# Gated attention stage: where a pair's projections and maxima stand among its sixteen units

## The reference

```
ss = sigmoid(x @ Ws).reshape(b, t, H, E); sd = sigmoid(x @ Wd).reshape(b, t, H, E)   # H = 8, E = 5
ss_g = ss * top3_mask(ss); sd_g = sd * top3_mask(sd)
q = sum over experts of (x @ Wq)[.., H, E, 64] * sd_g;  k, v likewise from Wkv with ss_g
attn = softmax(q k^T / 8);  out = attn v                       # per block b of 4 and head h of 8
y = sum over experts of (out @ Wo)[.., E, 128] * mask(sd)
```

## Time and profile before

| | |
|---|---|
| median of 3 runs | 4347.36 us |
| profiled execution | 4350.9 us, span 4349.2 us, mean granted clock 0.955 |
| PE busy | 3864.7 us (89%) |
| DVE busy | 3243.0 us (75%) |
| ACT busy | 1925.3 us (44%) |
| POOL busy | 2938.9 us (68%) |
| gated stage, units of pairs 0 to 15 | from 1282.3 to 2516 us of the span |

### The profile page before, as it was taken

One profiled execution on the slowest core, in us unless ns is written; L12 is line 12 of the kernel. 1 busy time (PEld: TensorE's weight loads), 2 busy tenths in 40 slices (PEclk: granted clock), 3 DMA queues, 4 the chain that ended last, 5 costly groups with the idle time before them and its releaser, 6 DMA issues. The chain is left out here.

```text
span 4349.2 us, 63343 instructions
## 1 busy us (share of the span) xinstructions
PE 3864.7 (89%) x22554; PEld 2205.7 (51%) x22554; DVE 3243.0 (75%) x5670; ACT 1925.3 (44%) x3478; POOL 2938.9 (68%) x2166
## 2 busy tenths in 40 slices
PE   7999999999788889899899848999999999999964
PEld 4555555555455555555555424555455444545533
DVE  6876878868487777877876648887888788878826
ACT  3443444434355455455455313444444444434423
POOL 3776767667536777877787835777677677767740
PEclk8999999999889999999999968999999999999987
DMA  3000100000010000100100021221222121212121
GB/s 55 21 22 1 38 14 25 10 6 1 27 59 20 28 19 28 38 19 28 33 28 10 6 59 30 41 34 30 39 32 43 30 40 30 43 22 44 19 59 30
DMA packets 98073, 125.90 MB, mean 29 GB/s; under 512 B 28928, under 2 KB 76480, under 8 KB 97760
## 3 DMA queue, kind: packets, MB, share of 16 engines
q1 hardware_dynamic: 97760, 121.86, 13.2%
HBM read 103.69 MB, written 18.12 MB: 28 GB/s over the span
## 5 line engine op out<-in xcount | busy, mean ns | idle before, releaser
L845 POOL TENSOR_TENSOR s_psum_p<-s_psum_p,s_prob 128x1024 f32<-128x1024 f32 (+3 forms) x640 | 1336.9, 2089 | 387.0 <-ACT s_prob L550 336.7
L550 ACT ACTIVATE s_prob<-s_sT 128x1024 f32<-128x1024 f32 (+2 forms) x896 | 792.0, 931 | 842.9 <-DVE s_sT L701 474.1
L449 PE MATMUL s_pv<-s_prob,s_vp 128*64 128x512 f32 (+3 forms) x3584 | 798.9, 567 | 3.9 <-POOL s_prob L830 3.9
L657 DVE CUSTOM_DVE_ANT_0 s_mx<-s_mx,s_strip 128x512 f32<-128x512 f32 x628 | 422.0, 714 | 161.8 <-PE s_mx L406 159.1
L1734 POOL TENSOR_TENSOR s_psum_p<-s_psum_p,s_prob 128x1024 f32<-128x1024 f32 x192 | 462.1, 2407 | 108.0 <-ACT s_prob L1457 106.2
L1457 ACT ACTIVATE s_prob<-s_sT 128x1024 f32<-128x1024 f32 x256 | 262.7, 1026 | 581.5 <-PE s_sT L1321 581.4
L706 DVE RECIPROCAL s_recip<-s_recip 128x128 f32<-128x128 f32 x512 | 452.7, 922 | 34.8 <-ACT s_recip L497 34.8
L406 PE MATMUL s_mx<-s_bh,s_ah 64*128 64x512 f32 (+2 forms) x1756 | 396.7, 447 | 87.2 <-DVE s_bm L647 39.0
L845 POOL TENSOR_TENSOR s_psum_p<-s_prob 128x1024 f32<-128x1024 f32 (+1 forms) x128 | 288.1, 2251 | 204.7 <-ACT s_prob L550 202.0
L449 PEld LDWEIGHTS s_pv<-s_prob,s_vp 128*64 128x64 f32 x3584 | 219.3, 137 | 369.0 <-issue 289.2
L647 DVE TENSOR_REDUCE s_bm<-s_mx 128x6 f32<-128x768 f32 (+2 forms) x376 | 360.0, 957 | 53.3 <-PE s_mx L406 44.6
(11 more groups left out here) (291 smaller groups left out, 7418.7 us busy)
## 6 DMA issues: line engine op xcount, KB each, us to landing
s_strip<-bias_rows SPq DMA_DIRECT2D x256, 144.0 KB, 5.8
s_wr<-gated_weights SPq DMA_DIRECT2D x32, 960.0 KB, 4.9
s_near<-bias_rows SPq DMA_DIRECT2D x256, 48.0 KB, 2.0
x<-s_x SPq DMA_DIRECT2D x10, 512.0 KB, 3.2
s_x<-x SPq DMA_DIRECT2D x8, 512.0 KB, 4.7
gated_weights<-s_side_hi SPq DMA_DIRECT2D x8, 480.0 KB, 2.6
gated_weights<-s_side_lo SPq DMA_DIRECT2D x8, 480.0 KB, 2.9
s_x<-in_L_attn_x_dram SPq DMA_DIRECT2D x4, 512.0 KB, 5.4
```

Of the source, the lines that this page charges most:

```text
L449: last = mm(pv[heads(hd), lo:CH], vp[:, g % 2, j, heads(hd)], prob[:, k % PR, hd, lo:CH], start=j == 0, stop=end)
L550: nc.scalar.activation(prob[:, k % PR, :, lo:CH], sT[:, k % 2, :, lo:CH], ACT.Exp, scale=st.scale).then_inc(exp_done, 1)
L657: last = nc.vector.tensor_tensor_reduce(out=mx[:, hd, :], in0=mx[:, hd, :], in1=strip[:, g % 2, hd, first:first + CH], scale=1.0, scalar=N ...
L845: nc.gpsimd.tensor_tensor(out[:, :, lo:CH], src, p[:, :, lo:CH], ALU.add)\
```

## The change

Both counts are rewritten: two projection steps in each of units 0 to 7, and maxima steps one each in units 4 and 5 and two each in units 8 to 14. The transposition of the maxima goes from unit 14 to unit 15 and stands right behind the scores there. In a unit, the projections now come ahead of the first maxima step, on TensorE and on VectorE, and no maxima step borrows a score buffer any more. The masked products of the first half (zp 0 to 3) go from units 12 to 15 to units 13, 14, 15 and 15. The gating of the next block (gx, gl) goes from units 6 to 9 to units 12 to 15; the ranking, which was in six groups of three or more operations spread over two pairs, is cut into 16 steps of one operation, all in the ranked pair from unit 5 on. The layer norm's steps move by one to three units.

```
--- before.py
+++ after.py
@@ -52,7 +52,7 @@
 ROWS = 16
 NROW = P // ROWS
 RINGP = 5
-TOPS, TOPC = E0 + 1, 8 + 3 * (E0 - 1)
+TOPS, TOPC = 4 + 3 * (E0 - 1), 8 + 3 * (E0 - 1)
 
 
 class Pairs:
@@ -939,8 +939,9 @@
 
     def __init__(self, name, scale):
         super().__init__(name, False, False, scale)
-        self.mx_steps = [0] * 4 + [1] * 6 + [2, 2, 3, 3, 0, 0]
-        self.pj_steps = [2] * 4 + [1] * 8 + [0] * 4
+        self.mt_unit = 15
+        self.mx_steps = [0] * 4 + [1, 1, 0, 0] + [2] * 7 + [0]
+        self.pj_steps = [2] * 8 + [0] * 8
         self.NP = HF // 2
         self.GP = B * self.NP
 
@@ -969,17 +970,16 @@
                 out[3 + i].append(("zp", g - 1, i))
         out[10].append(("rs", 2 * g))
         out[11].append(("zt", g, 0))
-        for i in range(4):
-            out[12 + i].append(("zp", g, i))
+        for i, u in enumerate((13, 14, 15, 15)):
+            out[u].append(("zp", g, i))
         gated, ranked = {0: 1, 3: 2, 7: 3}.get(g), {1: 1, 4: 2, 8: 3}.get(g)
         if gated is not None:
-            for u, job in ((6, ("gx", gated, 0)), (7, ("gx", gated, 1)), (8, ("gl", gated, 0)),
-                           (9, ("gl", gated, 1)), (10, ("top", gated, 0)), (11, ("top", gated, 1)),
-                           (14, ("top", gated, 2))):
+            for u, job in ((12, ("gx", gated, 0)), (13, ("gx", gated, 1)), (14, ("gl", gated, 0)),
+                           (15, ("gl", gated, 1))):
                 out[u].append(job)
         if ranked is not None:
-            for k, u in enumerate((8, 9, 11)):
-                out[u].append(("top", ranked, 3 + k))
+            for n, u in enumerate((5, 5, 6, 7, 8, 8, 9, 9, 10, 11, 11, 12, 12, 13, 14, 15)):
+                out[u].append(("top", ranked, n))
         if p == 0 and b > 0:
             for u, job in ((6, ("gt", b - 1, 0)), (7, ("gt", b - 1, 1)), (8, ("gt", b - 1, 2)),
                            (9, ("gt", b - 1, 3)), (12, ("y", b - 1, 0)), (13, ("gt", b - 1, 4)),
@@ -992,7 +992,7 @@
         if p == 1 and b + 1 < B:
             for k in range(2):
                 out[12 + k].append(("xs", b + 1, k))
-        for n, (of, u) in enumerate(((1, 13), (1, 14), (1, 15), (2, 2), (2, 3), (2, 6), (2, 7))):
+        for n, (of, u) in enumerate(((1, 15), (1, 15), (2, 4), (2, 5), (2, 6), (2, 6), (2, 9))):
             if p == of and b > 0:
                 out[u].append(("ln", b - 1, n))
         return out
@@ -1351,11 +1351,13 @@
                 scores(g, u, k, c, j)
                 steps = [t for t in todo if t[0] == "pj"]
                 chunks = [t for t in todo if t[0] == "mx"]
-                early = 1 if steps else 2
-                for t in chunks[:early]:
-                    maxima(t[1], t[2], second(todo, t, k))
+                early = 1
+                if ("mt", g + 1) in todo:
+                    m_transpose(g + 1)
                 for n, t in enumerate(steps):
                     project(t[1], t[2], k if n == 0 else None)
+                for t in chunks[:early]:
+                    maxima(t[1], t[2])
                 for t in todo:
                     if t[0] in GMISC:
                         misc_job(t)
@@ -1363,8 +1365,6 @@
                     values(k - 2)
                 for t in chunks[early:]:
                     maxima(t[1], t[2])
-                if ("mt", g + 1) in todo:
-                    m_transpose(g + 1)
             for k in range(GP * U - 2, GP * U):
                 values(k)
             for t in ending:
@@ -1575,34 +1575,36 @@
                 dve.wait_ge(xh_done, 2 * b + c + 1)
                 tt(xl[:, half(c)], xT[:, half(c)], f32(xh[:, half(c)]), ALU.subtract).then_inc(xl_done, 1)
 
-            def top_experts(b, k):
+            def top_experts(b, n):
 
                 gates, kept = gate[:, b % 2, :, :], keep[:, :, :]
-                at = TOPC * b + E0 + 3 * (k - 1)
-                if k == 0:
+                k, part = divmod(n + 2, 3)
+                if n == 0:
                     dve.wait_ge(sig_done, 2 * b + 2)
                     for e in range(E0):
                         nc.vector.memset(kept[:, e, :], float(E0 - 1 - e)).then_inc(top_step, 1)
-                elif k < E0:
+                    return
+                dve.wait_ge(top_step, TOPC * b + E0 + n - 1)
+                if k < E0:
                     later, earlier, won = slice(k, E0), slice(0, E0 - k), beats[:, 0:E0 - k, :]
-                    dve.wait_ge(top_step, at)
-                    tt(won, gates[:, earlier, :], gates[:, later, :], ALU.is_ge).then_inc(top_step, 1)
-                    dve.wait_ge(top_step, at + 1)
-                    tt(kept[:, later, :], kept[:, later, :], won, ALU.add).then_inc(top_step, 1)
-                    dve.wait_ge(top_step, at + 2)
-                    tt(kept[:, earlier, :], kept[:, earlier, :], won, ALU.subtract).then_inc(top_step, 1)
+                    if part == 0:
+                        ins = tt(won, gates[:, earlier, :], gates[:, later, :], ALU.is_ge)
+                    elif part == 1:
+                        ins = tt(kept[:, later, :], kept[:, later, :], won, ALU.add)
+                    else:
+                        ins = tt(kept[:, earlier, :], kept[:, earlier, :], won, ALU.subtract)
+                elif part == 0:
+                    ins = nc.vector.tensor_scalar(kept, kept, float(TOP) - 0.5, None, ALU.is_lt)
+                elif part == 1:
+                    ins = tt(gates, gates, kept, ALU.mult)
                 else:
-                    dve.wait_ge(top_step, at)
-                    nc.vector.tensor_scalar(kept, kept, float(TOP) - 0.5, None, ALU.is_lt)\
-                        .then_inc(top_step, 1)
-                    dve.wait_ge(top_step, at + 1)
-                    tt(gates, gates, kept, ALU.mult).then_inc(top_step, 1)
                     if b >= 2:
                         dve.wait_ge(share_done, 2 * NP * (b - 1))
-                    nc.vector.tensor_copy(
+                    ins = nc.vector.tensor_copy(
                         keep_d[:, b % 2, :, :, :],
-                        kept.rearrange("p e (i s h) -> p e i s h", i=NB, s=2)[:, :, :, 1, :])\
-                        .then_inc(top_step, 1)
+                        kept.rearrange("p e (i s h) -> p e i s h", i=NB, s=2)[:, :, :, 1, :])
+                ins.then_inc(top_step, 1)
+                if n == TOPS - 1:
                     dve.wait_ge(top_step, TOPC * (b + 1))
                     dve.sem_inc(top_done, 1)
 
@@ -1683,19 +1685,19 @@
                     misc_job(t)
                 steps = [t for t in todo if t[0] == "pj"]
                 chunks = [t for t in todo if t[0] == "mx"]
-                early = chunks[:1] if steps else chunks[:2]
-                for t in early:
-                    maxima(t[1], t[2], second(todo, t, k))
+                early = chunks[:1]
+                if ("mt", g + 1) in todo:
+                    max_rows(g + 1)
                 for n, t in enumerate(steps):
                     project(t[1], t[2], k if n == 0 else None)
+                for t in early:
+                    maxima(t[1], t[2])
                 for t in todo:
                     if t[0] == "mx":
                         if t not in early:
                             maxima(t[1], t[2])
                         if t[2] == NMX - 1:
                             head_maxima(t[1])
-                    elif t[0] == "mt":
-                        max_rows(t[1])
                     elif t[0] == "ln":
                         layer_norm(t[1], t[2])
                     elif t[0] == "zp":
```

## The result

The changed kernel takes 4498.9 us (median; 4496.8 to 4503.4) beside 4349.1 for the kernel before on the same chip: ratio 1.034, 95% interval 1.0325 to 1.0358, slower by 150 us. The prediction was 4431, range 4362 to 4490. The direction and the main wait are as forecast; the time lies above the range.

The account below looks back on a forecast made before the run. It began from PE, busy 89% of the span. Pairs with projections +92, extra jobs -18 and clock +10 gave +84 on 4350.9, so 4435; the median, 3.5 lower, made 4431 us, range 4362 to 4490.

Parts of the forecast that it names:

- Units 4 and 5: Maxima wait behind the second projection for its banks until 6.15, 2.3 us of idle PE; units last 8.0 and 9.2.
- Units 8 to 15: Two maxima steps per unit in 8 to 14 through one bank pair, at least 3.84 each; sum 33.0 against 34.4.
- Units 6 and 7: Two projections, scores and values, without waits for the borrowed score buffer: 4.87 us each.
- The border: Unit 0 of the next pair starts projections late behind two masked products: +0.9 us (0 to 2.2).
- the strict reading: VectorE and GpSimd exclude each other at every masked product, making unit 0's +0.9 a 2.2.
- The plain pair: Pair 11, which carries no extra jobs: 82.4 us, +6.6; +92 over the 14 pairs with projections.
- Extra jobs: Gating and ranking -11, block change and layer norm -7, partly hidden: together -18 us (-35 to +5).
- the signs that I had named: Profile signs: PE waits over 2 us twice a pair, given unit times, pairs 1 and 4 no longer far above neighbours.
- The clock: Falls of PE's clock behind 28 new waits of 2.3 us: +10 us (0 to 50).
- The clock rival: Granted clock falls for half of units 8 to 14, +1.5 us a unit: 4505 us; chance 0.13.
- The small loss: Low ends of the plain pair with most ranking hidden: 4358, up to 4390 us; chance 0.19.
- The faster case: PE the only bound, VectorE freeing the second projection's banks by 3.86 in units 4 and 5: 4300 us; chance 0.08.

Follow-up runs that it names:

- the kernel with filled row sums: Changed kernel plus nine unused 512-column matmuls in the wait of units 4 and 5 and five ahead of every row sum, units 5 and 10: 4471.2 us.
- the first experiment: Changed kernel with the maxima step ahead of the projections again, on TensorE and VectorE: 4381.0 us, ratio 1.007.
- the kernel with three steps: Changed kernel with maxima ahead of projections, one each in units 4-7, then 3, 2, 1, 1, 3, 2, second of three borrowing; products in units 12-15: 4325.7 us.
- the changed kernel with its waits filled: Changed kernel plus nine unused 512-column matmuls between the projections and the maxima step of units 4 and 5: 4459.9 us, ratio 1.025.

## Why the prediction was right in its direction and too low in its size

**Units 4 and 5: right.** 6.15 for the start of the maxima was 6.09, 2.3 of idle PE was 2.06 and 2.03 (the view counts these gaps from the modelled end of a matmul), unit 4's 8.0 was 8.09 where the clock stayed. Unit 5's 9.2 was 9.35 once the fillers' 1.15 is taken from the 10.50 of the kernel with filled row sums. Turned round, the order gave this back, with the clock behind it.

**Units 8 to 15: right in the mechanism, a little high.** Units 12 and 13 last 3.82 for 3.84. The banks turn as said, 1.91 from matmuls to matmuls; the timeline of pair 11 around the start of unit 12 answers the earlier trace rows:
```profile
2358.83 0.50 PE L1286 MATMUL s_mx<-s_bh,s_ah 64*128 64x512 f32 x2 [0.51 <-DVE s_bm L1616]
...
2359.37 1.23 DVE L1616 TENSOR_REDUCE s_bm<-s_mx 128x2 f32<-128x1024 f32 x1 [0.69 <-PE s_mx L1286]
...
2360.74 0.50 PE L1286 MATMUL s_mx<-s_bh,s_ah 64*128 64x512 f32 x2 [0.49 <-DVE s_bm L1616]
```
Units 8 to 15 of pair 11 add up to 32.8 with a fall in unit 10, 31.7 without (5.23 there, the 6.38 of the filled kernel less 1.15); 33.0 was said. What was too high is unit 8, where the banks are free at its start (3.28 instead of the 3.84 that I had called the least), and unit 11 (4.64 instead of 5.3). The low end that I gave for these units, 30.6, is 30.8 by its own terms. Units 6 and 7 last 5.21 and 4.95 (said 4.87), so scores hardly wait for a borrowed buffer there.

**The border: too low.** Unit 0 went to 7.2, +1.8, where +0.9 was taken; 0 to 2.2 was the bound. The stall at the border is the one described, a chain of projections starting late behind two masked products, and I took less than half of the strict reading. The Trainium skill (SBUF — State Buffer, Who interferes with whom) has a VectorE instruction with two SBUF inputs contend with a GpSimd one that reads SBUF, the shared port being an exclusive lock. The 4.40 of the two products beside an addition of 2.97, which takes 2.4 as a rule, agrees, and here the strict reading's 2.2 was nearer than my 0.9.

**The plain pair: nearly right, in part by luck.** Without falls pair 11 takes 82.8 (86.7 less 2.8 in unit 5 and 1.1 in unit 10), +7.0 where +6.6 was said. The +0.9 that was missing at the border and the 1.3 too much in units 8 to 15 cancel. In four of the pairs unit 1 lasts 6.3 to 7.4 instead of 5.4, behind a late unit 0; the kernel with all fillers has it in pair 11 too, and that pair without the fillers' 2.3 is 84.3, +8.5. Times 14 that is 98 to 119 for 92.

**Extra jobs: hidden about as well as said, or better.** The 82 us that stay with the clock as before, less 98 to 119 for the plain pairs and about 0 to 5 for pairs 14 and 15, leave -16 to -42 for them (82 - 98 and 82 - 119 - 5); -18 was said, -35 the bound. This is what is left over when the other terms are taken away, not a measurement of its own. Gating and ranking moved alone gain 22 in the kernel before, clock included. Of the signs that I had named, pair 4 is now no longer than its neighbours (94.9 beside 91.2 and 95.2), but pair 1 still is (93.1 beside 81.2 and 86.5): part of its excess stays, unit 14 with 6.52 instead of 4.18 in the median among it. (Of the seven layer norm steps one stayed in its unit and one moved by five units, to the next pair; the others by one to three.)

**The clock: the step that failed.** With its own terms the prediction had 92 - 18 = +74 before the clock, and the runs have +80 to +82. For the clock it had "+10 (0 to 50)", and the runs have 68 to 73. I had worked out the 50 (a third of pair 4's loss for each of 28 waits) and then put it down, because not each wait would bring a fall and part would be hidden. Nearly each did: of 28 such units 4 and 5, 25 have one. The trace of before could have said so: PE is idle for 1.8 us or more at a stretch 14 times in its gated stage, and 11 of these have a fall in them or within 3 us behind. Nor was it hidden, since behind a fall stood PE's own work on the path, the row sums and values of unit 5. And one term was missing: over the 14 pairs units 5 lost 34 us, units 4 18 and units 10 21 by the difference to the kernel with all fillers, the fillers' time taken away (the other units together differ by -5). The last of these was in my term nowhere, and units 4 and 5 alone are 51, just above the 50: the price of one was right, the discount was not. 82 + 68 = 150.

**The clock rival: right in its total, wrong in its place.** It put the loss in the pauses of units 8 to 14 and came to 4505. But units 12 and 13 kept their clock, and the falls sit where the row sums stand behind a maxima step, in units 5 and 10, and behind the long wait in unit 4. That its total of 4505 is within 6 us of the time is luck. Of the Trainium skill (TensorE: Matmul & The Clock Gate, A second HAM failure mode: psum-queue depth-cycling) I had said that it speaks most against the change. The clock did go back and forth, 48 times in the stage. But the micro-idles between groups, which the page makes the cause, are here the bank turns, and these alone brought few falls: in units 8, 12 and 13 of the changed kernel none begins.

**The rivals on the other side.** The small loss needed ends that did not come together: the ranking hid well, but the border went to its upper end. The faster case turned on the end of VectorE's second projection, and the order of the first experiment, which takes that wait away, shows how near it was: with it alone the kernel is still 31 us slower. With the maxima spread over more units and the products moved back as well it is faster than the kernel before.

**Left open.** Which unit 10 has a fall and which has none, with the same instructions in it (eight to eleven of sixteen in four of the kernels); why row sums directly behind a maxima step go with a fall and behind a projection hardly ever; how the hidden part of the extra jobs divides between ranking and layer norm; and whether another spread of the masked products would spare units 13 and 14.

## What to carry to other kernels

Before a step is put behind another on the same banks, read in the trace when the last reader frees them, and count all that queues behind: here 2.1 us twice a pair. Then price the pause twice, once as a wait and once as a fall of TensorE's clock behind it, and look at what PE has to do at that place; where falls had followed 11 of 14 long waits in the trace of before, they followed 25 of 28 new ones. A change with several parts held a gain of 22 us and losses of 118 and 37, each seen only when its part was undone or run alone (they need not add up: together 133 of the 150).

## What the runs showed of the hardware that was not expected

The granted clock fell inside stretches in which PE is shown busy throughout: those with 16 matmuls of one column each. They count as 1.8 to 3.0 us of busy PE, yet with five 512-column matmuls (1.15 us) between them and the maxima step ahead of them the falls in units 10 went from 11 to 1 in the kernel with three steps and from 14 to 3 in the changed kernel with its waits filled, and there from 10 to none in units 5. In unit 5, directly behind a projection, the same row sums saw one fall in 130 units of ten kernels. A busy share near 1 is no sign that the clock holds; the column of the granted clock has to be read beside it.

Matmuls whose results nobody uses paid for themselves: 18 us of them, and the time did not change beyond the noise. The lower level cost 0.36 to 0.38 us for each microsecond spent in it, where PE's work alone, at half its pace throughout, would lose 0.5; how the rest divides between waits that last as long at either level and other work was not measured.
